# Row maxima of an attention kernel by a scattered transfer instead of a transpose on TensorE

## The reference

```python
xn = layernorm(x)                                  # x is [4, 1024, 128]
Q, K, V = xn @ Wq, xn @ Wk, xn @ Wv                # 16 heads of 64
attn = softmax(Q K^T / 8)                          # per head, over 1024 keys
s = xn + gelu(attn V) @ Wpost
g = silu(mx_dequant(mx_quant(xn)) @ mx_dequant(mx_quant(w)).T + bias)   # blocks of 32
out = x + s * g
```

## Time and profile before

| | us |
|---|---|
| median of 3 runs | 1502.68 (1502.22 to 1504.25) |
| the profiled execution, its time | 1504.28 |
| its span | 1502.5 |
| busy: TensorE matmul, GpSimd, VectorE, ScalarE | 1456.3, 1144.7, 1080.7, 804.7 |

### The profile page before, as it was taken

The page is one execution under the profiler, slowest core; times in us unless marked ns, Lnnn a source line. Parts: engine busy times, 40 slices in busy tenths (PEclk is TensorE's granted clock), DMA queues, the critical chain, the costliest instruction groups (busy, mean ns, idle before and its releaser), DMA issues.

```text
span 1502.5 us, 25748 instructions
## 1 busy us (share of the span) xinstructions
PE 1456.3 (97%) x10369; PEld 794.2 (53%) x10369; DVE 1080.7 (72%) x1408; ACT 804.7 (54%) x1123; POOL 1144.7 (76%) x545
## 2 busy tenths in 40 slices
PE   5999999999999999999999999999999999999988
PEld 2555455555555555555555554555555555555478
DVE  6577777777777777777777777777777777777632
ACT  3455564555556565455555655555555555555563
POOL 0778788878887887887888778788778878877930
PEclk9999999999999999999999999999999999999999
DMA  2000000000000000000000000000000000002361
GB/s 76 1 8 15 8 15 29 16 8 15 15 8 15 15 13 24 15 14 8 15 15 15 8 15 14 9 15 15 8 15 8 1 1 1 1 1 80 118 220 49
DMA packets 25589, 35.40 MB, mean 24 GB/s; under 512 B 1792, under 2 KB 15872, under 8 KB 25472
## 3 DMA queue, kind: packets, MB, share of 16 engines
q1 hardware_dynamic: 25472, 33.76, 6.4%
HBM read 19.07 MB, written 14.68 MB: 22 GB/s over the span
## 4 chain that ended last, share of the span: by engine, by line
PE 88%; DVE 10%; issue 1%; ACT 1%; DMA 0%; POOL 0%; SPq 0%; ACTq 0%
PE acc L397 26%; PE scores L384 21%; PE peaks L368 11%; PE extra L287 8%; PE scores L388 7%; DVE half_maxes L807 5%; PE extra L317 4%; PE extra L300 4%; PE scores L456 4%; PE extra L324 2%; PE extra L338 1%; DVE extra L782 1%; DVE extra L783 1%; DVE extra L784 1%; DVE quant L785 1%
## 5 line engine op out<-in xcount | busy, mean ns | idle before, releaser
L696 POOL TENSOR_TENSOR prob_sum<-prob_sum,probs 128x1024 f32<-128x1024 f32 x384 | 912.1, 2375 | 236.7 <-ACT probs L571 209.3
L807 DVE TENSOR_REDUCE half_maxes<-peaks 128x2 f32<-128x1024 f32 x504 | 611.5, 1213 | 282.4 <-PE peaks L368 281.2
L571 ACT ACTIVATE probs<-scores 128x1024 f32<-128x1024 f32 x512 | 497.2, 1023 | 385.3 <-PE scores L388 375.4
L397 PE MATMUL acc<-probs,vals 128*64 128x512 f32 x2048 | 487.9, 597 | 0.0
L397 PEld LDWEIGHTS acc<-probs,vals 128*64 128x64 f32 x2048 | 137.2, 137 | 246.3 <-issue 218.1
L823 DVE RECIPROCAL inv_sum<-inv_sum 128x128 f32<-128x128 f32 x256 | 240.1, 941 | 0.0
L368 PE MATMUL peaks<-k_hi,q_hi 64*128 64x512 f32 x1008 | 226.0, 443 | 0.0
L384 PE MATMUL scores<-q_hi,k_hi 64*128 64x512 f32 x1024 | 202.7, 392 | 0.0
L388 PE MATMUL scores<-max_rows,ones_r 64*128 64x512 f32 x1024 | 202.2, 390 | 0.0
L384 PE MATMUL scores<-q_hi,k_lo 64*128 64x512 f32 x1024 | 202.1, 390 | 0.0
L384 PE MATMUL scores<-q_lo,k_hi 64*128 64x512 f32 x1024 | 202.0, 390 | 0.0
(11 more groups left out here) (147 smaller groups left out, 1025.6 us busy)
## 6 DMA issues: line engine op xcount, KB each, us to landing
att_scratch<-att SPq DMA_DIRECT2D x48, 256.0 KB, 2.0
probs<-att_scratch SPq DMA_DIRECT2D x8, 512.0 KB, 9.1
xTs<-att_scratch SPq DMA_DIRECT2D x4, 512.0 KB, 7.9
out_dram<-xn SPq DMA_DIRECT2D x8, 256.0 KB, 4.1
x_in<-in_L_attn_X SPq DMA_DIRECT2D x3, 512.0 KB, 4.0
q_hi_back<-att_scratch SPq DMA_DIRECT2D x2, 512.0 KB, 4.2
q_lo_back<-att_scratch SPq DMA_DIRECT2D x2, 512.0 KB, 5.0
k_hi_back<-att_scratch SPq DMA_DIRECT2D x2, 512.0 KB, 6.6
```

The costliest lines, as they stand in the source:

```text
L397: last = mm(acc[own[h], :], vals[(s // 2) % 2][:, j, own[h]], probs[j][:, h, :], start=(j == 0), stop=(j == KT - 1), tile_position=col[h])
L571: sa.activation(probs[j][:, :, :], scores[j % 2][:, :, :], ACT.Exp, scale=DH ** -0.5).then_inc(probs_ready, 1)
L696: gp.tensor_tensor(prob_sum[s % 2][:, :, :], before[:, :, :], probs[j][:, :, :], ALU.add).then_inc(probs_summed, 1)
L807: v.tensor_reduce(half_maxes[:, :, f // 2, f % 2], peaks[:, :, :], AX.X, ALU.max).then_inc(peaks_read, 1)
```

## The change

The fills for step `s + 1` are made earlier: fills 0 to 3 in rounds 2 and 3 of step `s - 1`, fills 4 to 7 in rounds 0 and 1 of step `s`. In step 0, which has nothing ahead of it, all eight fills for step 1 stand in rounds 0 and 1, four a round. `join_maxima` stands in round 1 and writes SBUF. SyncE then stores the 128 by 8 maxima into HBM transposed, one element at a time (1024 elements of 4 bytes, consecutive elements of a partition 512 bytes apart), waits for that, and loads two rows of 512 elements back, one into partition 0 and one into partition 64 of `max_rows`, whose other partitions are zero; the product subtracts them with a matrix of minus ones. `turn` and `spread_rows` are left for step 0 alone. TensorE's fourth product of a step waits for the loads instead of for `spread_rows`. The reciprocals are spread over the rounds of two steps, the quantisation goes in four parts instead of two, and GpSimd's `normalise` of an even step stands after its seventh sum instead of its fifth. SyncE's loads of stored halves near the end stand between these transfers: four of them ahead of the transfer for step 62, four behind it, and the others behind the transfer for step 63.

```diff
--- before.py
+++ after.py
@@ -24,6 +24,7 @@
     QBK = 4
     LN_EPS, Q_EPS, Q_MAX, QB = 1e-5, 1e-30, 7.5, 32
 
+    max_d = nc.dram_tensor("max_scratch", (2, HALF // P, P), F32, kind="Internal").ap()
     att_d = nc.dram_tensor("att_scratch", (NP, P, S), F32, kind="Internal").ap()
     x_t = x.rearrange("b (t p) d -> p (b t) d", p=P)
     out_t = out.rearrange("b (t p) d -> p (b t) d", p=P)
@@ -54,9 +55,15 @@
             before.append(("den", s - 1))
         if r == 2 and half == 1:
             before.append(("quant", n))
-        if r == 3 and s + 1 < NS:
-            behind.append(("turn", s + 1))
         return before, behind
+
+
+
+    def fills(s, r):
+        if s == 0 and r < 2:
+            return [(1, 4 * r + i) for i in range(4)]
+        at = (s + 1, 2 * r + 4) if r < 2 else (s + 2, 2 * r - 4)
+        return [(at[0], at[1] + i) for i in (0, 1)] if at[0] < NS else []
 
     FILLS = [("v", 0, 0), ("v", 0, 1), ("turn", 0)]
     for s in range(NS):
@@ -85,7 +92,9 @@
         q_hi_back, q_lo_back, k_hi_back = ([sb(f"{n}_back{z}", [P, S]) for z in (0, 1)] for n in ("q_hi", "q_lo", "k_hi"))
         k_lo_back = [sb(f"k_lo_back{z}", [P, S]) for z in (0, 1)]
         rows_back = [sb(f"rows_back{z}", [P, HALF]) for z in (0, 1)]
-        ones_r = sb("ones_r", [P, P], F32R)
+        first_rows = sb("first_rows", [P, HALF], F32R)
+        maxima = sb("maxima", [P, 2, QT])
+        ones_r, minus_r = sb("ones_r", [P, P], F32R), sb("minus_r", [P, P], F32R)
         vals = [sb(f"vals{z}", [P, KT, P]) for z in (0, 1)]
         probs = [sb(f"probs{k}", [P, 2, HALF]) for k in range(KT)]
         prob_sum = [sb(f"prob_sum{z}", [P, 2, HALF]) for z in (0, 1)]
@@ -150,7 +159,7 @@
         first_filled = sem("first_filled")
         extra_filled, extra_read = sem("extra_filled"), sem("extra_read")
         peaks_filled, peaks_read = sem("peaks_filled"), sem("peaks_read")
-        maxima_ready = sem("maxima_ready")
+        maxima_ready, max_stored, max_loaded = sem("maxima_ready"), sem("max_stored"), sem("max_loaded")
         highs_ready, lows_ready = sem("highs_ready"), sem("lows_ready")
         scores_ready, probs_ready, probs_summed = sem("scores_ready"), sem("probs_ready"), sem("probs_summed")
         pv_done, acc_read = sem("pv_done"), sem("acc_read")
...
@@ -222,18 +231,36 @@
             def load_x_back(c):
                 sp.dma_start(x_back[c].rearrange("p (t d) -> p t d", d=D), x_t[:, c * TC:(c + 1) * TC, :]).then_inc(x_loaded_back[c], 16)
 
+
+            def turn_maxima(s):
+                sp.wait_ge(maxima_ready, s + 1)
+                above(sp, max_loaded, 32 * (s - 1))
+                sp.dma_start(max_d.rearrange("h t p -> p (h t)"), maxima[:, :, :].rearrange("p h t -> p (h t)"),
+                             allow_slow_non_contiguous=True).then_inc(max_stored, 16)
+                sp.wait_ge(max_stored, 16 * s)
+                above(sp, scores_ready, KT * (s - 1))
+                for h in (0, 1):
+                    sp.dma_start(max_rows[s % 2][h * DH:h * DH + 1, :].bitcast(F32),
+                                 max_d[h:h + 1, :, :].rearrange("a t p -> a (t p)")).then_inc(max_loaded, 16)
+
             load_next_x(1)
-            for s in range(2, 2 * (NP - HP) + 2):
+            for s in range(NS - 1):
                 n, half = s // 2, s % 2
                 if half == 1 and n % HP == 4 and n // HP + 2 < B:
                     load_next_x(n // HP + 2)
-                store_att(s - 2)
-            for k in range(HP):
-                sp.wait_ge(stored[k], 32 * (B - 1))
-            is_filled(sp, ("v", NP - 1, 1))
-            sp.wait_ge(var_summed, part_of(B - 1, 0) + 1)
-            for p in range(HP):
-                load_att(p)
+                if s == NS - 3:
+                    for k in range(HP):
+                        sp.wait_ge(stored[k], 32 * (B - 1))
+                    is_filled(sp, ("v", NP - 1, 1))
+                    sp.wait_ge(var_summed, part_of(B - 1, 0) + 1)
+                    for p in range(HP // 2):
+                        load_att(p)
+                turn_maxima(s + 1)
+                if s == NS - 3:
+                    for p in range(HP // 2, HP):
+                        load_att(p)
+                if 1 < s < 2 * (NP - HP) + 2:
+                    store_att(s - 2)
             sp.dma_start(wp, wpost.rearrange("(h p) d -> p h d", p=P)).then_inc(wp_loaded, 16)
             sp.wait_ge(scores_ready, KT * (NS - 2))
             sp.wait_ge(pv_done, KT * (NS - 2))
@@ -361,8 +388,8 @@
             def peak(s, f):
                 n, z = s // 2, (s // 2) % 2
                 t, keys = (s % 2) * QT + f // 2, halves[f % 2]
-                if s % 2 == 0 and f == 0:
-                    pe.wait_ge(highs_ready, 4 * n + 4)
+                if s % 2 == 0 and f < 2:
+                    pe.wait_ge(highs_ready, 4 * n + 3 + f)
                 above(pe, peaks_read, 8 * s + f)
                 for h in (0, 1):
                     last = mm(peaks[:, h, :], q_hi[z][own[h], t * P:(t + 1) * P], k_hi[z][own[h], keys],
@@ -382,10 +409,13 @@
                 for left, right, begins in ((k_hi, q_hi, True), (k_hi, q_lo, False), (k_lo, q_hi, False)):
                     for h in (0, 1):
                         mm(w[:, h, :], left[z][own[h], ks], right[z][own[h], qs], start=begins, stop=False, tile_position=row[h])
-                if j == 0:
-                    is_read(pe, ("turn", s))
+                if j == 0 and s == 0:
+                    is_read(pe, ("turn", 0))
+                elif j == 0:
+                    pe.wait_ge(max_loaded, 32 * s)
+                sign, rows = (minus_r, max_rows[s % 2]) if s > 0 else (ones_r, first_rows)
                 for h in (0, 1):
-                    last = mm(w[:, h, :], ones_r[own[h], :], max_rows[s % 2][own[h], :], start=False, stop=True, tile_position=row[h])
+                    last = mm(w[:, h, :], sign[own[h], :], rows[own[h], :], start=False, stop=True, tile_position=row[h])
                 last.then_inc(scores_ready, 1)
 
             def weigh(s, j):
@@ -429,12 +459,13 @@
             for s in range(NS):
                 for r in range(4):
                     before, behind = extras(s, r)
-                    if s + 1 < NS:
-                        peak(s + 1, 2 * r)
+                    todo = fills(s, r)
+                    for at in todo[:1]:
+                        peak(*at)
                     score(s, 2 * r)
                     score(s, 2 * r + 1)
-                    if s + 1 < NS:
-                        peak(s + 1, 2 * r + 1)
+                    for at in todo[1:2]:
+                        peak(*at)
                     for use in before:
                         run(use)
                     if r > 0:
@@ -443,8 +474,12 @@
                     elif s > 0:
                         weigh(s - 1, 6)
                         weigh(s - 1, 7)
+                    for at in todo[2:3]:
+                        peak(*at)
                     for use in behind:
                         run(use)
+                    for at in todo[3:]:
+                        peak(*at)
             weigh(NS - 1, 6)
             weigh(NS - 1, 7)
 
...
@@ -694,7 +732,7 @@
                         pool.wait_ge(probs_summed, 7 * s + j - 1)
                     before = probs[0] if j == 1 else prob_sum[s % 2]
                     gp.tensor_tensor(prob_sum[s % 2][:, :, :], before[:, :, :], probs[j][:, :, :], ALU.add).then_inc(probs_summed, 1)
-                    if j == 5 and s > 1:
+                    if j == (7, 5)[s % 2] and s > 1:
                         normalise(s - 2)
             normalise(NS - 2)
             normalise(NS - 1)
@@ -761,7 +799,7 @@
                 blocked = lambda a: a.rearrange("p (c q) -> p c q", q=QB)
                 spread = lambda a: a[:, tile, :].unsqueeze(2).broadcast_to([P, QBK, QB])
                 word = lambda a: a.bitcast(mybir.dt.int32)
-                done = [before + (5 if src is not None else 4) * part]
+                done = [before + (0, 3, 5, 8)[part] + (part > 0 and src is not None)]
 
                 def step(ins):
                     ins.then_inc(quant_step, 1)
@@ -776,12 +814,14 @@
                     step(v.tensor_tensor(word(g), word(q), word(exponent[:, :]).broadcast_to([P, D]), ALU.bitwise_and))
                     step(v.tensor_scalar(h, g, 1.0, 0.0625, ALU.max, ALU.mult))
                     step(v.scalar_tensor_tensor(g, h, BIG, q, ALU.mult, ALU.add))
+                elif part == 1:
                     step(v.scalar_tensor_tensor(f, h, -BIG, g, ALU.mult, ALU.add))
-                else:
                     step(v.tensor_tensor(q, q, f, ALU.subtract))
+                elif part == 2:
                     step(v.tensor_tensor(q, q, h, ALU.add))
                     step(v.scalar_tensor_tensor(q, q, 0.0, h, ALU.is_le, ALU.mult))
                     step(v.scalar_tensor_tensor(g, q, -2.0, f, ALU.mult, ALU.add))
+                else:
```

(56 more changed lines are left out.)

7 lines of the change are left out of this document (5 added, 2 removed).

## The result

The changed kernel takes 1516.62 us (median; 1514.51 to 1520.82), the kernel before, run beside it, 1502.72 us (1502.22 to 1504.54). The ratio is 1.0088, with a 95% interval of 1.0078 to 1.0099: it is **slower by 0.9%**, a small loss but clear of the noise, where 1466.1 us and "faster" had been forecast. The profiled execution has a span of 1515.6 us at a granted clock of 0.993.

The account below looks back on a forecast made before the run. TensorE, busy 97%, bounds the kernel; 40.1 us won at step ends less 3.5 net for step 0 gives 36.6, so 1502.68 becomes 1466.1 us. Own range 1462 to 1472, 8 in 10 reaching to 1483; forecast's chance 0.77.

Parts of the forecast that it names:

- the scattered store's price: Store of 1024 4-byte packets to HBM: 4.0 us, bounds 2.0 and 16, taken from the load of x.
- The rest of the chain: After the store: 0.5 us for three wake-ups, 2.2 for a load to land, 0.5 for issuing the second.
- The budget: Time from join in round 1 to fourth product: 11.0 us in an odd step, about 13.5 in an even one.
- break-even: Transfer chain of 12.2 us, a store of 9.0 us or 0.14 us a packet, eats the whole gain.
- (b): Rival: slow store, fourth product waits; chain L costs (L - 11.0) + (L - 13.5) a step pair; up to 1911 us; chance 0.07.
- (c): Rival: rows in time for even steps, a little late for odd; L 11.0 to 12.2, 1466 to 1503 us; chance 0.05.
- `turn` and the wait: At step ends, removing TensorE's turn and its wait for the join wins 31.5 plus 8.6, 40.1 us.
- Step 0: Eight fills through one buffer in two rounds lose 4.6 us; step 62 wins 1.1 back; net cost 3.5 us.
- Worth nothing: Moving quantisation, reciprocals and normalise was priced at no gain or cost, since TensorE shows no gap there.
- rival (a): TensorE runs into VectorE in rounds 2 and 3 of odd steps; 0.4 us each, 26 us, so 1492; chance 0.11.
- The 1.8 us of slack: Even step's normalise, moved behind two sums, ends 1.8 us before ScalarE's copy needs its buffer; no cost.
- The loads at the end: Four 512 KB loads ahead of step 62's transfer delay its store by 2 to 4 us once, costing nothing or little.

Follow-up runs that it names:

- e4: Kernel before plus awaited transfers of several forms that nothing depends on; 1024 elements stored side by side took 8.4 to 11.2 us, each on its own line 2.9.
- e7: Kernel before plus awaited, unneeded stores of 1024 4-byte elements to HBM at distances of 4 to 256 bytes; 10.0 us at 4 bytes, 2.7 at 64.
- e10: Kernel before plus awaited, unneeded transfers of 1024 or 128 4-byte elements; to HBM side by side 10.4 and 7.1 us, 128 at 64 bytes 1.4.
- e5: Changed kernel with the scratch elements in HBM 64 bytes apart and rows loaded element by element; 1473.32 us, ratio 0.9796 to the kernel before.
- e9: e5 with reciprocals, quantisation and normalise back near their old places; 1483.03 us, ratio 0.986 to the kernel before.
- e8: e6 with GpSimd's normalise of the last two steps two sums earlier; 1472.1 us, ratio 0.9783 to the kernel before.
- e1: Changed kernel storing 256 runs of 16 bytes instead of 1024 of 4, TensorE reading the row with a 16-byte step; 1589.12 us, ratio 1.056.
- e6: e5 with step 0's fills spread three a round over its rounds; 1473.31 us.

## Why the prediction was wrong

**The step that failed** is the scattered store's price: 4.0 us, taken from the load of x because that has as many packets. It measured 9.7, and with it TensorE's fourth product waits in nearly every even step, where the forecast had it hidden with 3.8 us to spare. The row taken reads from HBM in pieces of 512 bytes; the store writes pieces of 4 bytes side by side into it. e4 shows that the direction decides (3.0 us to read 1024 single elements), e7 and e10 that the distance does. The count, the one thing that the row was chosen for, matters far less: 1024 elements 64 bytes apart take 2.7 us, 128 side by side 7.1. The range of the term, 2.0 to 16, held the value near its middle; the choice within it, and the small chance given to its upper half, did not follow from any row. The rest of the chain, put at 3.2 us, took some 2.6 (12.2 less a store of 9.6 in those steps).

**The budget and the break-even were right.** 11.0 us were forecast between join and fourth product of an even step, and 11.0 are measured. Rows made in even steps were given 13.5; in e5, where nothing waits, it is 13.4, and there is no wait in the odd steps 3 to 61: 20.17 us in both the change and e5. Not seen was that this budget shrinks at the ends: from join to product e5 has only 9.8 us in step 1 and 10.5 in step 63, and there the odd steps wait too. By the formula of rivals (b) and (c), even steps of 23.72 instead of 22.49 us mean L = 11.0 + 1.23 = 12.2 us, exactly the point named as break-even, and the step pair is 43.9 us, hardly another than the 43.6 before. The store was put at 9.0 us there. So the mechanism is that of rivals (b) and (c), at the border between them, to which 0.12 had been given together. The total lies 12 us above the 1466.1 + 38 that (b)'s formula gives there: 7 of them are missing in e5 as well (below), and the other 5 come mostly from steps 1 and 62, whose waits are longer and have slower products behind them.

**The Trainium skill**, "DMA: Bandwidth & Descriptors" (Rules for kernel authors, and Specifications), had spoken against the change. It was right in the direction; the prediction had drawn from it a time nearer to the upper bound of 16 us, and the 9.7 lie about midway between that and the 4.0 taken. Its one descriptor per element agrees with the packets under 512 bytes (67438 in the changed kernel, 1792 before). But e5 has twice as many (133840) and is fast, so the count in that rule is not what costs here. Its section "Why small descriptors are slow (HBM only)" says that SBUF to SBUF doesn't suffer; the 2.3 us of e4's `el_sb` agree. It sets HBM apart as a whole, and there this case differs: single elements read from HBM (2.2 to 3.0 us) or written 64 bytes apart (2.7) were as quick.

**`turn` and the wait** were put at 40.1 us. In e5 steps 1 to 61 are 35.2 us shorter (0.8 + 34.4). A pair takes 42.66 us, forecast 42.6, so that 0.92 is won instead of 1.00, and 6.8 us instead of 8.6 come from the long waits. The mechanism was right, the term 4 to 5 us too large.

**Step 0** was put at 4.6 us lost and measured 5.2, and 1.1 us came back in step 62 as said. Not seen was step 1 of the change: it is the first to use transferred rows, waits 2.46 us, and its products stand apart behind the wait.

**"Worth nothing" was wrong twice.** The moves of reciprocals, quantisation and `normalise` are worth 9.7 us against e9's arrangement. The argument had been that no gap showed in the trace of before. In that trace the five operations of the quantisation stand in round 3, and the reduction behind them ends just ahead of `turn`:

```profile
1088.39 0.29 DVE L785 TENSOR_TENSOR quant<-extra,blk_max 128x128 f32<-128x128 f32 x1
1088.60 1.22 DVE L807 TENSOR_REDUCE half_maxes<-peaks 128x2 f32<-128x1024 f32 x1
```

It ends at 1089.82; without `turn` the next fill could start at 1087.89 + 1.86 = 1089.75. So what the five operations cost was hidden in the wait for the join and the time of `turn` at the step's end. In e9, with five in round 2 and no `turn`, it shows as 0.20 us an odd step. That is the mechanism of rival (a), TensorE waiting for VectorE at a fill, at a quarter of its 0.8 us. With the old split of four and five it would by these rows be about 0.1 us, an estimate; no run has it. And `normalise` behind two sums, said to cost nothing, holds up the last copy of the kernel by 3.3 us; moving it back brings that copy 0.8 us nearer (e8). The 1.8 us of slack came from a step that isn't the last.

**The loads at the end** were said to delay the transfer of step 62 by little. Step 62 takes 3.9 us more than in e5: its product waits 1.91 us, and the window around it has the lower level of the clock again:

```profile
1405.00:1412.00 7.00, 5.09 (x24) 1.83 (x20) 3.88 (x4) 2.05 (x2) 5.82 (x3) 0.76 0.83 300
```

DMA was busy for 0.83 of it, at 300 GB/s, with the four loads behind the transfer. The product starts 13.1 us behind the join, where the other even steps take 11.7 to 12.9 and 12.2 in the mean, so the loads' part of the wait is some 0.9 us at most; the store itself took 10.2 us, in its usual range. What four loads ahead of the store can cost is seen in e5: 5.9 us instead of 2.8, so 3.1 more, inside the 2 to 4 forecast, and hidden there.

With the store mended, the forecast of 1466.1 us meets 1473.3: 4.9 us short at the step ends, 0.6 in step 0 and about 0.9 behind the last step, less 0.8 at the start; and the 1.6 us by which the profiled execution of before lay above its median, which e5's doesn't.

## What to carry to other kernels

Price a transfer by a row that agrees in direction, place and spacing of its pieces, before one that agrees in their count; where none does and the budget lies inside the bounds, give the costly side real weight, or measure the transfer idle in the kernel before. Elements of 4 bytes that must be written to HBM one by one are put 64 bytes apart, and the load picks them up: here that alone turned 0.9% slower into 2.0% faster. When a pause is taken out of a bound engine, look at which other engine's late work it covered: here five operations ahead of a reduction.

## What the runs showed of the hardware

- Writing 1024 elements of 4 bytes to HBM took 10.0 us side by side, 4.4 at 8 bytes, 3.3 at 16, 2.9 at 32 and 2.7 at 64 (medians, e7 and e10); 128 side by side took 7.1, and 1.4 at 64 bytes. Eight elements of one partition inside 64 bytes, 8 bytes apart, took 5.95 for 1024 (e4). Reading 1024 such elements took 2.2 to 3.0 us, SBUF to SBUF 2.3 (e4).
- A moving operand of 64x512 read with a step of 16 bytes nearly halves TensorE's rate: products 0.44 us apart instead of 0.23 at the full clock (e1). The Trainium skill, "Advanced Engine Details and Errata" (SBUF Cachelines), describes lines of 16 bytes and a penalty where each access meets another one; the row fits that, but no run here tried another step.
- Around waits of 2.46 us (step 1) and 1.91 us (step 62) the granted clock averaged 0.76 over 7 us; behind one of 1.56 us in a step between, products stood 0.23 us apart as ever. At the end, waits of 3.92 us (e6) and 3.15 us (e8) of TensorE were followed by 12 us windows with 0.72 and 1.00 in them.
